# Fusion attention: the normalised input written by VectorE in one subtract-and-multiply, in place of ScalarE's scaled identity and GpSimd's product

## The chip, the core and the metric

The kernel runs on one core of a Trainium2 chip. The metric is the device time of one execution in microseconds. Engines are named as in the profile: PE (TensorE), with PEld for its weight loads, DVE (VectorE), ACT (ScalarE), POOL (GpSimd), SP (SyncE, which here only issues transfers).

## The reference

A batch of 64 samples. Each gives 128 image rows and 77 text rows of 64 numbers, `h` of shape 64 x 205 x 64. Then one attention layer and one layer of experts are added to it:

```python
h = jnp.concatenate([image_branch(x), text_branch(x_txt)], axis=1)        # (64, 205, 64)
h = h + attn(_layernorm(h), Wq, bq, Wk, bk, Wv, bv, Wo, bo)
h = h + ffn(_layernorm(h), W1, b1, Wg, bg, Wd, bd)

def _layernorm(x, axis=-1, eps=1e-05):
    m = jnp.mean(x, axis=axis, keepdims=True)
    v = jnp.var(x, axis=axis, keepdims=True)
    return (x - m) / jnp.sqrt(v + eps)

def attn(x, ...):            # 4 heads of 16
    q, k, v = heads(x @ Wq.T + bq), heads(x @ Wk.T + bk), heads(x @ Wv.T + bv)
    a = softmax(einsum('bhnd,bhmd->bhnm', q, k) * 16 ** -0.5)
    out = einsum('bhnm,bhmd->bhnd', a, v).transpose(0, 2, 1, 3).reshape(B, N, C)
    return out.astype(bfloat16).astype(float32) @ Wo.T + bo
```

The change is in `_layernorm(h)` ahead of the attention layer, and nowhere else.

## The kernel before

Four stages follow one another, each with its own block of instruction streams: image branch, text branch, fusion attention, experts. All of `h` stays in SBUF, as `h_img` (128 rows x 64 samples x 64) and `h_txt` (77 rows).

Fusion attention (`fusion_attention`) handles one sample a step, in a software pipeline over 64 samples: step `n` works on four samples at once. Every engine has a `step` function, and the order in which the code stands there is the order in which the engine runs it; engines are held together by semaphores alone. In step `n`:

- sample `n+3` is normalised. DVE takes means and variances of the two tiles (128 image rows, 77 text rows) with `set_stats`: `at_mean_var`, then `at_neg_mean` and `at_var_eps`. POOL makes `at_rstd` by a power of -0.5 and `at_neg_mean_rstd`, the product of the two (`set_scale`). ACT writes `at_z` = h * rstd + (-mean * rstd), one instruction a tile (`norm_rows`, line 1517). ACT then copies `at_z` rounded into `at_xs` (L1838), and POOL writes the rest, `at_z` minus that (L1780).
- sample `n+2` is projected. PE turns `at_xs` into the bank `at_work`, ACT copies it to `at_xT` (L1819), PE multiplies by `at_wk` and `at_wq` (L1891, four projections, two banks). For each projection ACT cuts a low part, `at_qk_lo` (`part_lo`, L1802), and DVE takes it off again with the bias, `at_KF` twice and then `at_QF` twice (`cut_qk`, L1701). POOL spreads each `at_KF` over the heads as `at_KB` (L1774). PE projects V behind the first `at_QF` (`project_v`, L1899).
- sample `n+1` has its scores and their row maxima (`at_mpad`, L1683), turned by PE into `at_maxT`, from which DVE makes `at_QP` (`join_max`, L1691).
- sample `n` has its transposed scores (L1865), the exponentials `at_PT` (L1792, two of them), the weighted sum `at_outT` (L1912), copied by ACT as `at_oU` (L1830); sample `n-1` is projected by `at_wo` and added to `h`.

The places that matter are the middle of the step on ACT (`part_lo` 0 and 1, `norm_rows`, `at_oU`, `part_lo` 2 and 3) and on DVE (`cut_qk` 0 and 1, `join_max`, `cut_qk` 2 and 3), and PE's `project_v`, which waits for `qk_cut` of `cut_qk` 2. The steps run in a loop of two steps per pass.

Of the kernel before, what the change touches and what calls it, by code (L numbers as in the profile page):

```python
# [1459 lines left out]
def set_stats(dve, rows_of, mean_var, stats, neg_mean, var_eps, aggregated, var_ready, m, between=None):  # L1460

    for t, (_, n) in enumerate(TILES):
        dve.bn_stats(stats[0:n, t], rows_of(m, t))
    if between:
        between()
    dve.drain()
    for t, (_, n) in enumerate(TILES):
        last = dve.bn_aggr(mean_var[0:n, t], stats[0:n, t])  # L1468
    last.then_inc(aggregated, 1)
    dve.wait_ge(aggregated, m + 1)  # L1470
    dve.tensor_scalar(neg_mean[:], mean_var[:, :, 0], -1.0, None, ALU.mult)
    dve.tensor_scalar(var_eps[:], mean_var[:, :, 1], EPS, None, ALU.add).then_inc(var_ready, 1)


# [47 lines left out]
def fusion_attention(p, inputs, ident, rows_of):  # L1522
# [8 lines left out]
    with ExitStack() as ctx:  # L1531
        def sb(name, shape, dtype=F32):
            return ctx.enter_context(nc.sbuf_tensor("at_" + name, shape, dtype))
# [9 lines left out]

        stats, mean_var = sb("stats", [P, 2, 6]), sb("mean_var", [P, 2, 2])
        var_eps, rstd = sb("var_eps", [P, 2]), sb("rstd", [P, 2])
        neg_mean, neg_mean_rstd = sb("neg_mean", [P, 2]), sb("neg_mean_rstd", [P, 2])
        z = sb("z", [P, 2, D])
        xs = sb("xs", [P, 2, 2 * D], F32R)
        xT = sb("xT", [P, SEQP], F32R)
# [23 lines left out]
        with ExitStack() as setup:  # L1573
# [76 lines left out]
                        dve.tensor_scalar(cols[:, at + 2:at + 4], cols[:, at:at + 2], lo_rows[:, who:who + 1],  # L1650
                                          None, ALU.mult)

        aggregated, var_ready, rstd_ready, scale_ready, z_ready, x_hi, x_cut, x_turned, xT_set = (
            sem("aggregated"), sem("var_ready"), sem("rstd_ready"), sem("scale_ready"), sem("z_ready"), sem("x_hi"),
            sem("x_cut"), sem("x_turned"), sem("xT_set"))
        projected, lo_part, qk_cut, k_split, v_made, v_set = (
            sem("projected"), sem("lo_part"), sem("qk_cut"), sem("k_split"), sem("v_made"), sem("v_set"))
# [16 lines left out]
        with nc.Block() as block:  # L1674
            @block.vector
            def _(dve):
                def find_max(m, tile):

                    n = TILES[tile][1]
                    dve.wait_ge(scored, m * 2 + (tile + 1))  # L1680
                    if tile == 0 and due(m):
                        dve.wait_ge(max_turned, m)
                    dve.tensor_reduce(mpad[0:n, tile].rearrange("p t (j r) -> p t j r", r=A_GROUP)[:, :, :, 3 * A_DH],  # L1683
                                      scores[0:n, :, 0:A_HPT * SEQP].rearrange("p t (j s) -> p t j s", j=A_HPT)[:, :, :, 0:SEQ],
                                      AX.X, ALU.max, negate=True).then_inc(max_set, 1)

                def join_max(m, par):
                    dve.wait_ge(max_turned, m + 1)
                    if due(m * 2 - 2):
                        dve.wait_ge(scored_t, m * 2 - 2)  # L1690
                    dve.tensor_tensor(QP[:, par, :, 0:SEQ], maxT[:, :, 0:SEQ], QF[:, par, :, 0:SEQ].bitcast(F32),  # L1691
                                      ALU.add).then_inc(q_set, 1)

                def cut_qk(m, i, par):

                    t, is_q = i % 2, i // 2
                    dst = QF[:, par, t] if is_q else KF[:, t]
                    dve.wait_ge(lo_part, m * 4 + (i + 1))
                    if i == 0 and due(m * 2):
                        dve.wait_ge(k_split, m * 2)  # L1700
                    dve.scalar_tensor_tensor(out=dst, in0=work[(i + 1) % 2][:, 0:SEQP],  # L1701
                                             scalar=cols[:, (0 if is_q else 4) + t:(1 if is_q else 5) + t],
                                             in1=qk_lo[:, i % 2].bitcast(F32), op0=ALU.add, op1=ALU.subtract)\
                        .then_inc(qk_cut, 1)

                def set_v(m, par):
                    dve.wait_ge(v_made, m + 1)
                    if due(m - 1):
                        dve.wait_ge(weighed, m - 1)
                    for tile, (_, n) in enumerate(TILES):  # L1710
                        last = dve.tensor_tensor(
                            V[0:n, par, tile, :, 0:A_DH],
                            work[1][0:n, tile * D:(tile + 1) * D].rearrange("p (h c) -> p h c", h=A_HEADS),
                            bv[0:n].rearrange("p (h c) -> p h c", h=A_HEADS), ALU.add)
                    last.then_inc(v_set, 1)

                def normalise_o(m, par):
                    dve.wait_ge(outs_turned, m + 1)
                    if due(m - 1):
                        dve.wait_ge(o_turned, m - 1)  # L1720
                    dve.reciprocal(rsum[:], outs[:, :, :, A_DH]).then_inc(sums_inv, 1)
                    dve.wait_ge(sums_inv, m + 1)
                    dve.tensor_tensor(o_rows[:, par, :, 0:D].rearrange("p a (h c) -> p a h c", h=A_HEADS), outs[:, :, :, 0:A_DH],
                                      rsum[:].unsqueeze(3).broadcast_to([P, 2, A_HEADS, A_DH]), ALU.mult)\
                        .then_inc(o_set, 1)

                def add_y(m):
                    dve.wait_ge(y_made, m + 1)
                    for tile, (_, n) in enumerate(TILES):
                        last = dve.tensor_tensor(rows_of(m, tile), rows_of(m, tile),  # L1730
                                                 work[1][0:n, tile * D:(tile + 1) * D], ALU.add)
                    last.then_inc(y_added, 1)

                def step(n, par):
                    if live(n + 3):
                        if due(n + 3):
                            dve.wait_ge(scale_ready, n + 3)
                        set_stats(dve, rows_of, mean_var, stats, neg_mean, var_eps, aggregated, var_ready, n + 3,
                                  between=(lambda: find_max(n + 1, 0)) if live(n + 1) else None)
                    elif live(n + 1):  # L1740
                        find_max(n + 1, 0)
                    if live(n - 1):
                        add_y(n - 1)
                    if live(n + 1):
                        find_max(n + 1, 1)
                    if live(n + 2):
                        cut_qk(n + 2, 0, par)
                        cut_qk(n + 2, 1, par)
                    if live(n + 1):
                        join_max(n + 1, 1 - par)  # L1750
                    if live(n + 2):
                        cut_qk(n + 2, 2, par)
                        cut_qk(n + 2, 3, par)
                    if live(n):
                        normalise_o(n, par)
                    if live(n + 2):
                        set_v(n + 2, par)

                each_step(dve, step)

            @block.gpsimd
            def _(pool):
                def step(n, par):
                    if live(n + 3):
                        set_scale(pool, neg_mean, var_eps, power, rstd, neg_mean_rstd, var_ready, rstd_ready,
                                  scale_ready, n + 3)
                    if live(n + 2):

                        m = n + 2
                        if due(m * 2 - 2):  # L1770
                            pool.wait_ge(scored_t, m * 2 - 2)
                        for t in range(A_TENSORS):
                            pool.wait_ge(qk_cut, m * 4 + (t + 1))
                            pool.tensor_tensor(KB[:, par, t],  # L1774
                                               KF[:, t].bitcast(F32).unsqueeze(1).broadcast_to([P, A_HPT, SEQP]),
                                               head_rows[:].unsqueeze(2).broadcast_to([P, A_HPT, SEQP]), ALU.mult)\
                                .then_inc(k_split, 1)
                    if live(n + 3):
                        pool.wait_ge(x_hi, n + 4)
                        pool.tensor_tensor(xs[:, :, D:], z[:], xs[:, :, 0:D].bitcast(F32), ALU.subtract)\  # L1780
                            .then_inc(x_cut, 1)

                each_step(pool, step)

            @block.scalar
            def _(act):
# [18 lines left out]
                def step(n, par):  # L1805
# [9 lines left out]
                    if live(n + 2):  # L1815
# [3 lines left out]
                        act.activation(xT[:, 0:SEQ], work[0][:, 0:SEQ], ACT.Copy).then_inc(xT_set, 1)  # L1819
                        part_lo(n + 2, 0)  # L1820
                        part_lo(n + 2, 1)
                    if live(n + 3):
                        if due(n + 3):
                            act.wait_ge(x_cut, n + 3)
                        norm_rows(act, rows_of, z, rstd, neg_mean_rstd, scale_ready, z_ready, n + 3)
                    if live(n):
                        act.wait_ge(weighed, n + 1)
                        if due(n):
# [577 lines left out]
```

## Time and profile before

| | us |
|---|---|
| median of 3 runs | 2744.31 |
| lowest, highest | 2728.9, 2755.52 |
| the profiled execution | 2730.05 |
| its span, first to last instruction | 2728.2 |
| attention stage, first to last exponential and what lies about it | 1832 to 2316 |
| busy over the whole span: PE, DVE, ACT, POOL | 2268.2, 1892.6, 1453.0, 1243.7 |
| mean granted clock of PE | 0.905 |

The profile is of one execution, near the lowest of the three runs. A stretch's granted clock is a mean between 0.5 (1.2 GHz) and 1 (2.4 GHz). Busy times don't add up to the span since engines work side by side; what sets a stage's time has to be read from its waits.

### The profile page before, as it was taken

What the parts mean: (1) busy time and instruction counts of PE and PEld (TensorE: products, weight loads), DVE (VectorE), ACT (ScalarE), POOL (GpSimd) and SP (SyncE); (2) the same over time, 40 slices, a digit from 0 to 9 for tenths busy, and PEclk for the clock granted to TensorE, in tenths of its full rate; (3) what the DMA queues carried; (4) which work ended last, traced back from release to release, by engine and by line L of the source; (5) the groups of instructions that cost most, each with busy time, mean ns of one, the idle gap of its engine ahead of it and who ended that gap; (6) DMA issues with size and microseconds to landing.
All of it is one profiled execution on the core that took longest, in us unless ns stands there. A gap on an engine that the chain in (4) does not pass through costs nothing. (4 is left out here: it accounts for less than half of the span.)

```text
span 2728.2 us, 63210 instructions
## 1 busy us (share of the span) xinstructions
PE 2268.2 (83%) x19769; PEld 1792.5 (66%) x19769; DVE 1892.6 (69%) x6491; ACT 1453.0 (53%) x3500; POOL 1243.7 (46%) x1650
## 2 busy tenths in 40 slices
PE   5699999778886998778877888628888898699998
PEld 5699999666665776656665666526666665466665
DVE  3455565467866777668856776668888766588888
ACT  2122222136656665756665665746666656566663
POOL 2233333226646555656555654664444433434442
PEclk8899999869978999989987998859999969699999
DMA  4100000000000000000000000000000000000000
GB/s 118 29 13 16 12 17 6 1 1 1 0 1 1 2 0 0 1 3 0 0 1 2 1 0 1 1 0 0 0 0 0 0 0 0 4 10 9 8 9 11
DMA packets 38122, 19.09 MB, mean 7 GB/s; under 512 B 28045, under 2 KB 37389, under 8 KB 37903
## 3 DMA queue, kind: packets, MB, share of 16 engines
q1 hardware_dynamic: 38003, 17.64, 2.6%
q8 instruction: 58, 0.95, 0.2%
q14 instruction: 61, 0.50, 0.1%
HBM read 14.27 MB, written 3.36 MB: 6 GB/s over the span
## 5 line engine op out<-in xcount | busy, mean ns | idle before, releaser
L444 PE MATMUL im_c<-im_a_hi,im_w 128*128 128x256 f32 (+2 forms) x1920 | 428.9, 318 | 47.0 <-POOL im_a_lo L341 47.0
L444 PEld LDWEIGHTS im_c<-im_a_hi,im_w 128*128 128x128 f32 x1920 | 321.2, 191 | 63.5 <-POOL im_a_lo L341 47.8
L1012 POOL TENSOR_TENSOR tx_KB<-tx_KF,tx_head_rows 128x1248 fp32r<-128x1248 f32 x128 | 288.1, 2271 | 52.1 <-DVE tx_KF L881 52.1
L444 PE MATMUL im_c<-im_a_lo,im_w 128*128 128x256 f32 (+2 forms) x960 | 304.1, 317 | 0.0
L830 POOL TENSOR_TENSOR tx_rstd<-tx_var_eps,tx_power 77x4 f32<-77x4 f32 x128 | 130.7, 1021 | 366.0 <-DVE tx_var_eps L826 366.0
L1080 ACT ACTIVATE tx_PT<-tx_scores_t 77x624 f32<-77x624 f32 x256 | 174.7, 682 | 219.1 <-PE tx_scores_t L1224 214.5
L1224 PE MATMUL tx_scores_t<-tx_QP,tx_KB 128*77 128x78 f32 x2048 | 206.5, 254 | 11.3 <-DVE tx_QP L901 6.3
L895 DVE TENSOR_REDUCE tx_mpad<-tx_scores 77x8 fp32r<-77x616 f32 x256 | 202.1, 790 | 11.2 <-PE tx_scores L1206 10.6
L1224 PEld LDWEIGHTS tx_scores_t<-tx_QP,tx_KB 128*77 128x77 f32 x2048 | 188.3, 161 | 30.8 <-DVE tx_QP L901 30.8
L334 POOL TENSOR_TENSOR im_rstd<-im_var_eps,im_power 128x4 f32<-128x4 f32 x64 | 68.7, 1074 | 304.7 <-DVE im_var_eps L262 304.7
L837 ACT ACTIVATE tx_yn<-tx_y,tx_neg_mean_rstd,tx_rstd 77x64 f32<-77x64 f32 x512 | 189.0, 433 | 6.7 <-POOL tx_neg_mean_rstd L832 6.7
L444 PEld LDWEIGHTS im_c<-im_a_lo,im_w 128*128 128x128 f32 x960 | 182.5, 190 | 8.3
L257 DVE BATCH_NORM_STATS2 im_stats<-im_h 128x6 f32<-128x128 f32 (+1 forms) x192 | 47.7, 304 | 185.0 <-ACT im_h L383 66.6
L2284 PE MATMUL ex_y<-ex_wd,ex_H_hi 128*128 128x512 f32 (+1 forms) x512 | 172.7, 419 | 0.0
L1073 ACT ACTIVATE tx_qk_lo<-tx_work,tx_cols,tx_lo_rows 128x312 fp32r<-128x312 f32 x258 | 143.1, 606 | 53.9 <-PE tx_work L1188 53.9
L1792 ACT ACTIVATE at_PT<-at_scores_t 128x824 f32<-128x824 f32 (+1 forms) x128 | 109.5, 856 | 106.3 <-PE at_scores_t L1865 106.3
L375 ACT ACTIVATE im_a_hi<-im_normed 128x192 fp32r<-128x192 f32 (+1 forms) x192 | 62.9, 348 | 192.9 <-DVE im_normed L280 190.9
L1774 POOL TENSOR_TENSOR at_KB<-at_KF,at_head_rows 128x412 fp32r<-128x412 f32 x128 | 109.3, 874 | 96.8 <-DVE at_KF L1701 96.8
L1683 DVE TENSOR_REDUCE at_mpad<-at_scores 128x4 fp32r<-128x820 f32 (+1 forms) x128 | 129.5, 1011 | 28.9 <-PE at_scores L1852 22.0
L1802 ACT ACTIVATE at_qk_lo<-at_work,at_cols,at_lo_rows 128x206 fp32r<-128x206 f32 x256 | 120.1, 519 | 54.6 <-PE at_work L1891 54.6
L1005 POOL TENSOR_TENSOR tx_xs<-h_txt,tx_xs 77x256 fp32r<-77x256 f32 x130 | 108.7, 836 | 70.6 <-ACT tx_xs L1061 68.9
L1179 PE MATMUL tx_work<-ident,tx_xs 128*128 128x128 f32 x516 | 92.9, 307 | 56.3 <-POOL tx_xs L1005 56.3
(286 smaller groups left out, 6027.1 us busy)
## 6 DMA issues: line engine op xcount, KB each, us to landing
im_x<-x SPq DMA_DIRECT2D x16, 384.0 KB, 3.4
out<-h_img SPq DMA_DIRECT2D x32, 64.0 KB
tx_toks<-x_txt SPq DMA_DIRECT2D x1, 1925.0 KB
im_raw<-L_tok_conv_w SPq DMA_DIRECT2D x1, 1280.0 KB, 8.7
out<-h_txt SPq DMA_DIRECT2D x32, 38.5 KB
im_raw<-L_tok_conv_w SPq DMA_DIRECT2D x1, 960.0 KB, 4.7
im_raw<-L_tok_conv_w SPq DMA_DIRECT2D x1, 640.0 KB, 5.9
tx_raw_W<-L_txt_W SPq DMA_DIRECT2D x2, 256.0 KB, 6.2
```

Source lines behind the costliest of these rows:

```text
L444: last = pe.matmul(acc[:, :, d0:d1], w[c][:, slot, part], img[:, b0_:b1_, d0 + shift:d1 + shift, kj:kj + J], start=opens, stop=closes)
L830: pool.tensor_tensor(rstd[:, par], var_eps[:, par], power[0:R], ALU.pow).then_inc(y_rstd, 1)
L837: last = act.activation(yn[:, par, b], y[:, par, b], ACT.Identity, bias=neg_mean_rstd[:, par, b:b + 1], scale=rstd[:, par, b:b + 1])
L895: dve.tensor_reduce(mpad[0:R].rearrange("p t (j r) -> p t j r", r=GROUP)[:, :, :, 3 * DH], scores[0:R, :, 0:HPT * SP_TXT].rearrange("p t ( ...
L1012: pool.tensor_tensor(KB[:, par, t], KF[:, t].bitcast(F32).unsqueeze(1).broadcast_to([P, HPT, QW]), head_rows[:].unsqueeze(2).broadcast_to( ...
L1073: act.activation(qk_lo[:, i % 2], work[(i + 1) % 2][:, 0:QW], ACT.Identity, bias=cols[:, at:at + 1], scale=lo_rows[:, 1 - is_q:2 - is_q]). ...
L1080: act.activation(PT[0:R, b % 2], scores_t[0:R, :, 0:HPT * SP_TXT], ACT.Exp, scale=SCALE)\
L1224: last = pe.matmul(scores_t[0:R, t, j * SP_TXT:(j + 1) * SP_TXT], k, QP[:, b % 2, t], start=True, stop=True)
L1683: dve.tensor_reduce(mpad[0:n, tile].rearrange("p t (j r) -> p t j r", r=A_GROUP)[:, :, :, 3 * A_DH], scores[0:n, :, 0:A_HPT * SEQP].rearra ...
L1792: act.activation(PT[0:n, tile], scores_t[0:n, :, 0:A_HPT * SEQP], ACT.Exp, scale=SCALE)\
L1802: act.activation(qk_lo[:, i % 2], work[(i + 1) % 2][:, 0:SEQP], ACT.Identity, bias=cols[:, at:at + 1], scale=lo_rows[:, 1 - is_q:2 - is_q] ...
L2284: last = pe.matmul(acc, h[:, slot, half, at:at + n], wd[:, part, half, 0:WIDE], start=False, stop=half == HALVES - 1 and h is H_lo)
```

## The change

DVE writes `at_z` with one TENSOR_SCALAR a tile: subtract the mean, multiply by `at_rstd`, both operands columns with one value a row. It stands in a new function `norm_z`, called behind `cut_qk(n + 2, 1, par)` and ahead of `join_max(n + 1, 1 - par)`. ACT's two instructions for `at_z` go, and so do POOL's `at_neg_mean_rstd`, DVE's `at_neg_mean` and the semaphore `scale_ready` in this stage. The experts stage still uses the old functions.

```diff
@@ set_stats
     dve.wait_ge(aggregated, m + 1)
-    dve.tensor_scalar(neg_mean[:], mean_var[:, :, 0], -1.0, None, ALU.mult)
+    if neg_mean is not None:
+        dve.tensor_scalar(neg_mean[:], mean_var[:, :, 0], -1.0, None, ALU.mult)
     dve.tensor_scalar(var_eps[:], mean_var[:, :, 1], EPS, None, ALU.add).then_inc(var_ready, 1)
@@ fusion_attention, DVE
+                def norm_z(m):
+                    dve.wait_ge(rstd_ready, m + 1)
+                    if due(m):
+                        dve.wait_ge(x_cut, m)
+                    for t, (_, n) in enumerate(TILES):
+                        last = dve.tensor_scalar(z[0:n, t], rows_of(m, t), mean_var[0:n, t, 0:1], rstd[0:n, t:t + 1],
+                                                 ALU.subtract, ALU.mult)
+                    last.then_inc(z_ready, 1)
@@ DVE, step
                     if live(n + 3):
-                        if due(n + 3):
-                            dve.wait_ge(scale_ready, n + 3)
-                        set_stats(dve, rows_of, mean_var, stats, neg_mean, var_eps, aggregated, var_ready, n + 3,
+                        set_stats(dve, rows_of, mean_var, stats, None, var_eps, aggregated, var_ready, n + 3,
                                   between=(lambda: find_max(n + 1, 0)) if live(n + 1) else None)
...
                         cut_qk(n + 2, 0, par)
                         cut_qk(n + 2, 1, par)
+                    if live(n + 3):
+                        norm_z(n + 3)
                     if live(n + 1):
                         join_max(n + 1, 1 - par)
@@ POOL, step
                     if live(n + 3):
-                        set_scale(pool, neg_mean, var_eps, power, rstd, neg_mean_rstd, var_ready, rstd_ready,
-                                  scale_ready, n + 3)
+                        pool.wait_ge(var_ready, n + 4)
+                        pool.tensor_tensor(rstd[:], var_eps[:], power[:], ALU.pow).then_inc(rstd_ready, 1)
@@ ACT, step
                         part_lo(n + 2, 0)
                         part_lo(n + 2, 1)
-                    if live(n + 3):
-                        if due(n + 3):
-                            act.wait_ge(x_cut, n + 3)
-                        norm_rows(act, rows_of, z, rstd, neg_mean_rstd, scale_ready, z_ready, n + 3)
                     if live(n):
                         act.wait_ge(weighed, n + 1)
```

DVE's order in the middle of a step of the loop, before. `at_KF` comes from `cut_qk` 0 and 1, `at_QP` from `join_max`, `at_QF` from `cut_qk` 2 and 3:

```order
L1468 BN_AGGR at_mean_var<-at_stats 77x2
L1471 TENSOR_SCALAR at_neg_mean<-at_mean_var 128x2
L1472 TENSOR_SCALAR at_var_eps<-at_mean_var 128x2
L1730 TENSOR_TENSOR h_img<-h_img,at_work 128x64
L1730 TENSOR_TENSOR h_txt<-h_txt,at_work 77x64
L1683 TENSOR_REDUCE at_mpad<-at_scores 77x4
L1701 SCALAR_TENSOR_TENSOR at_KF<-at_work,at_cols,at_qk_lo 128x206 x2
L1691 TENSOR_TENSOR at_QP<-at_maxT,at_QF 128x2x205
L1701 SCALAR_TENSOR_TENSOR at_QF<-at_work,at_cols,at_qk_lo 128x206 x2
```

And the same place of DVE in the changed kernel:

```order
L1701 SCALAR_TENSOR_TENSOR at_KF<-at_work,at_cols,at_qk_lo 128x206
L1722 TENSOR_SCALAR at_z<-h_img,at_mean_var,at_rstd 128x64
L1722 TENSOR_SCALAR at_z<-h_txt,at_mean_var,at_rstd 77x64
L1690 REGISTER_ALU
L1691 TENSOR_TENSOR at_QP<-at_maxT,at_QF 128x2x205
```

The two `at_z` now stand on DVE between the second `at_KF` and `at_QP`, and `at_neg_mean` is gone ahead of `at_var_eps`.

ACT's order at the same place of a step, before; `at_qk_lo` is `part_lo`:

```order
L1802 ACTIVATE at_qk_lo<-at_work,at_cols,at_lo_rows 128x206
L1515 REGISTER_ALU
L1517 ISA
L1517 ACTIVATE at_z<-h_img,at_neg_mean_rstd,at_rstd 128x64
L1517 REGISTER_ALU
L1517 ACTIVATE at_z<-h_txt,at_neg_mean_rstd,at_rstd 77x64
L1827 REGISTER_ALU
L1830 ACTIVATE at_oU<-at_outT 128x206
```

And in the changed kernel:

```order
L1811 ACTIVATE at_qk_lo<-at_work,at_cols,at_lo_rows 128x206
L1832 REGISTER_ALU
L1835 ACTIVATE at_oU<-at_outT 128x206
L1808 REGISTER_ALU
L1811 ACTIVATE at_qk_lo<-at_work,at_cols,at_lo_rows 128x206
```

On ACT `at_oU` follows the second `at_qk_lo` directly.

## Rows read from the trace of the kernel before

**Rows 1.** Windows of the attention stage: stretch, length, busy time, granted clock, DMA.

```profile
1832.00:2180.00 348.00, 292.64 (x2550) 212.50 (x2550) 282.41 (x898) 238.74 (x567) 143.99 (x236) 0.98 0.00 0
2180.00:2316.00 136.00, 120.71 (x867) 88.00 (x866) 91.92 (x284) 81.20 (x183) 44.52 (x72) 0.76 0.00 0
```

**Rows 2.** Waits, 1832 to 2316: total us, times, longest.

```profile
POOL at_KB L1774 <- DVE at_KF L1701: 94.3, 62, 4.8
...
PE at_work L1899 <- DVE at_QF L1701: 27.4, 62, 0.6
```

**Rows 3.** Timeline: start us, us, engine, line, instructions; one step.

```profile
2071.36 0.58 DVE L1691 TENSOR_TENSOR at_QP<-at_maxT,at_QF 128x410 fp32r<-128x410 f32 x1
...
2076.35 0.70 PE L1891 MATMUL at_work<-at_xT,at_wk 128*128 128x206 f32 x4 [0.27 <-ACT at_xT L1819]
...
2076.94 0.94 ACT L1802 ACTIVATE at_qk_lo<-at_work,at_cols,at_lo_rows 128x206 fp32r<-128x206 f32 x2 [0.64 <-PE at_work L1891]
...
2077.59 0.77 DVE L1701 SCALAR_TENSOR_TENSOR at_KF<-at_work,at_cols,at_qk_lo 128x206 fp32r<-128x206 f32 x2 [0.46 <-ACT at_qk_lo L1802]
2077.77 0.43 ACT L1517 ACTIVATE at_z<-h_img,at_neg_mean_rstd,at_rstd 128x64 f32 x1
...
2078.10 1.71 POOL L1774 TENSOR_TENSOR at_KB<-at_KF,at_head_rows 128x412 fp32r<-128x412 f32 x2 [1.38 <-DVE at_KF L1701]
2078.10 0.43 ACT L1517 ACTIVATE at_z<-h_txt,at_neg_mean_rstd,at_rstd 77x64 f32 x1
...
2078.17 0.71 PE L1891 MATMUL at_work<-at_xT,at_wq 128*128 128x206 f32 x4
2078.43 0.32 ACT L1830 ACTIVATE at_oU<-at_outT 128x206 f32<-128x206 f32 x1
2078.50 0.58 DVE L1691 TENSOR_TENSOR at_QP<-at_maxT,at_QF 128x410 fp32r<-128x410 f32 x1
2078.66 0.94 ACT L1802 ACTIVATE at_qk_lo<-at_work,at_cols,at_lo_rows 128x206 fp32r<-128x206 f32 x2
...
2079.22 0.84 DVE L1701 SCALAR_TENSOR_TENSOR at_QF<-at_work,at_cols,at_qk_lo 128x206 fp32r<-128x206 f32 x2
...
2079.71 0.55 PE L1899 MATMUL at_work<-at_wv,at_xT 128*128 128x64 f32 x4 [0.46 <-DVE at_QF L1701]
```

**Rows 4.** Like operations on DVE: a source view of L288, L699; timeline of L288.

```profile
L288 DVE TENSOR_SCALAR im_res<-im_h,im_mean_var,im_rstd x64: 339/342/347, 104.9 to 531.1; 128x128 f32<-128x128 f32 x64
...
L699 DVE TENSOR_SCALAR tx_hot<-tx_toks,tx_word_f x16: 367/367/372, 549.6 to 566.2; 100x308 f32 x14, 100x308 f32<-100x308 int32 x2
...
104.94 1.11 DVE L288 TENSOR_SCALAR im_res<-im_h,im_mean_var,im_rstd 128x128 f32<-128x128 f32 x4 [1.12 <-POOL im_rstd L334]
```

**Rows 5.** Source view of L1774: ns min/median/max.

```profile
L1774 POOL TENSOR_TENSOR at_KB<-at_KF,at_head_rows x128: 869/874/877, 1822.3 to 2305.0; 128x412 fp32r<-128x412 f32 x128
```

**Rows 6.** Source view of L825; timeline at 1117 us, DVE and POOL.

```profile
L825 DVE TENSOR_SCALAR tx_neg_mean<-tx_mean_var x128: 166/166/447, 611.8 to 1762.2; 77x4 f32<-77x4 f32 x128
...
1117.53 0.45 DVE L825 TENSOR_SCALAR tx_neg_mean<-tx_mean_var 77x4 f32<-77x4 f32 x1
...
1117.21 0.73 POOL L843 TENSOR_TENSOR tx_x_shift<-h_txt,tx_rows 77x256 f32<-77x256 f32 x1
```

**Rows 7.** Timeline at 32 us, DVE and POOL.

```profile
32.07 1.01 DVE L280 SCALAR_TENSOR_TENSOR im_normed<-im_scaled,im_rstd,im_b 128x192 f32<-128x192 f32 x2
...
32.30 2.15 POOL L341 TENSOR_TENSOR im_a_lo<-im_normed,im_a_hi 128x192 fp32r<-128x192 f32 x4 [1.24 <-ACT im_a_hi L375]
```

**Rows 8.** Timeline at 862 us, DVE and POOL.

```profile
862.13 0.16 DVE L826 TENSOR_SCALAR tx_var_eps<-tx_mean_var 77x4 f32<-77x4 f32 x1
...
862.12 0.75 POOL L1005 TENSOR_TENSOR tx_xs<-h_txt,tx_xs 77x256 fp32r<-77x256 f32 x1 [1.93 <-ACT tx_xs L1061]
```

**Rows 9.** Timeline of DVE in a stretch at half clock.

```profile
2241.09 0.59 DVE L1691 TENSOR_TENSOR at_QP<-at_maxT,at_QF 128x410 fp32r<-128x410 f32 x1
...
2248.44 0.77 DVE L1701 SCALAR_TENSOR_TENSOR at_KF<-at_work,at_cols,at_qk_lo 128x206 fp32r<-128x206 f32 x2 [0.30 <-ACT at_qk_lo L1802]
2250.61 0.58 DVE L1691 TENSOR_TENSOR at_QP<-at_maxT,at_QF 128x410 fp32r<-128x410 f32 x1 [1.40 <-PE at_maxT L1927]
2251.55 0.86 DVE L1701 SCALAR_TENSOR_TENSOR at_QF<-at_work,at_cols,at_qk_lo 128x206 fp32r<-128x206 f32 x2 [0.36 <-ACT at_qk_lo L1802]
```

More of the change, by code:

```diff
@@ L1545, in fusion_attention @@
         var_eps, rstd = sb("var_eps", [P, 2]), sb("rstd", [P, 2])
-        neg_mean, neg_mean_rstd = sb("neg_mean", [P, 2]), sb("neg_mean_rstd", [P, 2])
         z = sb("z", [P, 2, D])
@@ L1651, in _ @@
                                           None, ALU.mult)
-        aggregated, var_ready, rstd_ready, scale_ready, z_ready, x_hi, x_cut, x_turned, xT_set = (
-            sem("aggregated"), sem("var_ready"), sem("rstd_ready"), sem("scale_ready"), sem("z_ready"), sem("x_hi"),
+        aggregated, var_ready, rstd_ready, z_ready, x_hi, x_cut, x_turned, xT_set = (
+            sem("aggregated"), sem("var_ready"), sem("rstd_ready"), sem("z_ready"), sem("x_hi"),
             sem("x_cut"), sem("x_turned"), sem("xT_set"))
```

## The prediction

> **What bounds the kernel now.** Only the attention stage changes, so I read that stretch first, by the view of windows: from 1832 to 2316 us, 484 of the 2728.2, PE is busy 84% in the part at full clock and 89% in the part where the clock was partly granted at half, DVE 81% and 68%, ACT 69% and 60%, POOL 41% and 33% [rows 1]. No engine is full, so busy shares decide nothing: the stage is a cycle of waits. The view of waits shows two of its links, PE waiting for `at_QF` before the V projection 62 times, once a step, 27.4 us in all, and POOL idle 94.3 us before `at_KB` [rows 2].
>
> The timeline of one step gives the cycle [rows 3]. Two `at_QP` starts, 2071.36 and 2078.50, give its period, 7.14 us; the step that also closes the loop takes 7.36, by the same reading. Inside it PE's K projection starts at 2076.35, ACT's first `at_qk_lo` at 2076.94, DVE's `at_KF` pair at 2077.59, the `at_QF` pair at 2079.22, and PE's V projection at 2079.71, half a microsecond after `at_QF` began, with PE idle before it. Behind it PE issues in order the transposed scores, on which ACT's exponentials and the next `at_xT` wait. So whatever moves the start of `at_QF` moves the whole step.
>
> What holds `at_QF` now is ACT: `at_qk_lo` starts at 2078.66 and lasts 0.52 (two in 0.94), and `at_QF` starts 0.04 after its end. Just before it ACT runs without a gap: `at_qk_lo` pair, `at_z`, `at_z`, `at_oU`, `at_qk_lo` [rows 3]. Both rows of `at_z` are thus on the path as the row stands, which makes the change look like a gain. DVE's `at_QP` ends at 2079.08, 0.14 us before `at_QF`.
>
> **The change part by part.** ACT loses two `at_z` of 0.43 us, which start 0.33 apart: 0.66 us less in front of `at_qk_lo` [rows 3]. That buys nothing, because PE stands right behind. The third `at_qk_lo` needs the Wq projection, which starts at 2078.17, 0.49 us before it. For the first `at_qk_lo` the same distance is 0.59 us (2076.35 to 2076.94). PE itself issued Wq behind its own transposes. The bound from above is therefore 0 us, and from below a few hundredths; I take 0. POOL loses `at_neg_mean_rstd`, 0.20 us, at a time when it waits anyway: 0. DVE loses `at_neg_mean`, 0.17 us, in front of a `at_mpad` that waits for PE's scores: 0. The wait for `scale_ready` at the head of DVE's step had always been met: 0.
>
> DVE gains two TENSOR_SCALAR of 64 columns with two column operands, between the `at_KF` pair and `at_QP`. The nearest row is `im_res`, the same operation with 128 columns: 342 ns, four in 1.11 us, so (1.11 - 0.34) / 3 = 0.257 us apart [rows 4]. This class of operation takes in about two columns a cycle: `tx_hot` writes 308 columns in 367 ns, where `at_KF` needs 430 for 206 [rows 3, 4]. 64 columns fewer are 0.033 us less: an estimate of 0.31 us each, 0.22 apart. If nothing else held them, the first would start at 2078.27 (two `at_KF` of 0.43 in 0.77 us start 0.34 apart, so the second did at 2077.93, and the next can 0.34 later), the second at 2078.49, `at_QP` at 2078.71 in place of 2078.50, ending at 2079.29; back-to-back operations overlap by 0.08 to 0.09, so `at_QF` could start at 2079.21. Against 2079.22 that is nothing. This is the lower end.
>
> But they would not be alone. POOL begins the first `at_KB` at 2078.10, at the end of the first `at_KF`, and the two run to 2079.81 [rows 3]; one lasts 874 ns [rows 5], so the first ends at 2078.97. The trace shows what a TENSOR_SCALAR from SBUF to SBUF does while POOL works: `tx_neg_mean`, 166 ns at the median of 128, took 447 when it started 0.32 us into a 0.73 us product on POOL, and ended 0.04 us after that product, at 1117.98 against 1117.94 [rows 6]. So DVE stands still until POOL's instruction is over. The `at_z` pair comes inside `at_KB` in every step, because `at_KB` is released by the first `at_KF` and `at_z` by the second.
>
> How many of the two `at_KB` does it wait for? In the image part DVE's `im_normed` ran into four `im_a_lo` that POOL issues without a gap (32.30 to 34.45, 0.54 each) and had ended by 33.08, while the second was under way [rows 7]: a waiting DVE instruction slips in between two of POOL's. So the first `at_z` runs at 2078.97, ending at about 2079.03 (0.04 as there, and some 0.03 for the columns). The second has to be ready before POOL takes hold again. `tx_var_eps`, which started 0.01 us behind a POOL product, was not held (0.16 us) [rows 8]; so POOL takes hold about 0.15 us after its start, which here is 2078.93 + 0.15 = 2079.08. The second `at_z` is ready 0.22 after the first, at 2079.2: too late by 0.1 us. I take it to wait for the second `at_KB`, to 2079.81, and to end at 2079.87. `at_QP` follows at 2079.79 (overlap 0.08), ends at 2080.37, and `at_QF` starts at 2080.29 in place of 2079.22: **1.07 us a step**, all of it on the cycle.
>
> Beside these rows: the Trainium skill, SBUF — State Buffer, section Who interferes with whom, says that a `tensor_scalar` in a two-port mode and a GpSimd operation exclude one another, that whichever issued first keeps the pair of ports for its whole instruction, and that the other is fully blocked. No row here shows it for column operands. By the page's order of issue (first `at_z`, second `at_KB`, second `at_z`) the sum is 1.07 us as well; by busy times alone it would be 0.
>
> How many steps pay? Both sides of the wait are there in 62 steps [rows 2]. In the part at half clock PE is so late that the wait is covered: there `at_KF` starts at 2248.44, so `at_KB` would end 2.2 us later (as in rows 3) at 2250.66, while `at_QP` started only at 2250.61 behind PE's transposes, and `at_QF` at 2251.55 behind ACT [rows 9]. A step there costs 0 more. From 2180 to 2316 the mean clock was 0.76, which is 48% of 136 us, 65 us, at 1.2 GHz, and 0.98 over 348 us adds 14 [rows 1]; at about 10 us a step (2241.09 to 2250.61 is 9.5) that is 8 steps. 62 - 8 = 54 steps, by 1.07: **58 us**. Against the profiled execution's own 2730.05 us (span 2728.2 and 1.9 around it) that gives 2788. The three runs have their median 14 us higher, at 2744.31; put on that, 2802. I forecast 2800.
>
> **Rivals.**
> - *Not slower: DVE isn't held.* Column operands, or the strided `h_img` rows, might keep `at_z` on one port. Then `at_QF` starts at 2079.21 and nothing moves: 2744. For it: no row shows `im_res` under a POOL instruction. Against it: its 342 ns fit two columns a cycle, the class that was held. It decides below 0.2 us of waiting per step, the slack found above.
> - *Both slip in.* If POOL takes hold 0.1 us later than I read, both `at_z` end by 2079.25; `at_QP` starts at 2079.17, `at_QF` at 2079.67: 0.45 us by 54, 24 us, 2768.
> - *Both wait for the second `at_KB`.* 1.07 + 0.22 = 1.29 us by 54, 70 us: 2814.
> - *The clock gives back.* The mean granted clock was 0.98 up to 2180, with PE busy 84%, and stretches at 1.2 GHz came after that [rows 1]. With PE at 73% (84 by 7.25 / 8.32) these may not come: 62 steps pay 66 us, and 8 steps of 10 us fall back to 7.25, minus 22 to 24: +42, 2786.
> - *A gain.* It needs ACT's relief to reach `at_QF` and DVE to be free: at most 0.14 us by 62, 9 us, under the 1% (27 us) that a measurement of this kernel can tell.
>
> **How the numbers follow.** Main case 0.58, with the clock giving back 0.10, both waiting 0.07, both slipping in 0.10, not held 0.13, a gain 0.02. The range goes from 2755 (both slipping in, less half of the 27 us that the runs spread) to 2822 (both waiting, plus 8) and leaves out 0.15. Over 1% slower is above 2772: the first three cases and a little of the fourth, 0.77. Within 1%: 0.21. Faster by over 1%: 0.02.
>
> **What the changed profile would show.** DVE `at_z` with a median far above 0.31 us, the first ending 0.06 after the first `at_KB`, the second 0.06 after the second; `at_QP` to `at_QP` 8.2 and 8.4 us; ACT idle before its third `at_qk_lo` or right after it; PE idle over 1.5 us before the V projection in place of 0.46; POOL's `at_KB` still 874 ns. If both `at_z` last about 0.31 and steps stay at 7.14, the hold was misread. If one is short and one long the order in the gap is right. A different share of the half-speed clock would move the total by tens of microseconds without touching these.

## The result, and the profile after

The changed kernel takes 2857.65 us (median of 4 runs, 2853.64 to 2868.36), against 2736.61 for the kernel before (4 runs, 2724.39 to 2755.52): a ratio of 1.044, 95% interval 1.037 to 1.052. Every ratio here compares only the executions of each kernel that lie within 1.5% of its fastest, since the granted clock differs from one execution to the next. The kernel is slower, as forecast, but by 121 us where 56 were forecast, and above the range. The profiled execution, the slowest of the four, took 2868.36 us with a span of 2866.6, 138 us more than the span of before; the sums below are of the two profiled executions, and so add up to 138 and not to 121.

Where the time lies is read from windows. The view of one source line gives the stage's ends: the first and the last instruction of PE's output projection, which comes once a sample, start at 1845.8 and 2459.0 us, 613 us apart, where they started 475 apart before (1843.2 and 2318.6). The difference is 138 us, so all of it is in the attention stage. In the windows below (stretch, length, busy time of PE, PEld, DVE, ACT and POOL, granted clock) the stage's row answers to [rows 1]:

```profile
2097.40:2107.30 9.90, 6.82 (x64) 5.08 (x62) 8.86 (x25) 6.01 (x14) 4.11 (x7) 1.00 0.00 0
2107.50:2118.00 10.50, 10.25 (x56) 7.64 (x56) 7.56 (x22) 4.81 (x10) 2.51 (x4) 0.50 0.00 0
1832.00:2459.00 627.00, 576.64 (x3424) 426.47 (x3424) 459.86 (x1246) 301.83 (x628) 176.08 (x247) 0.60 0.00 0
```

The granted clock of the stage is 0.60, where [rows 1] had 0.98 and 0.76 for its two parts. At 0.60, 80% of 627 us, some 500 us, ran at 1.2 GHz. The first two rows are a little over one step at each level. The fall at the end of the first of them came just after PE had stood still for 1.6 us.

That step, at 2.4 GHz, answers to [rows 3]. DVE's rows first, then POOL's, ACT's and PE's of the same stretch:

```profile
2098.21 0.57 DVE L1691 TENSOR_TENSOR at_QP<-at_maxT,at_QF 128x410 fp32r<-128x410 f32 x1
...
2104.20 0.77 DVE L1701 SCALAR_TENSOR_TENSOR at_KF<-at_work,at_cols,at_qk_lo 128x206 fp32r<-128x206 f32 x2 [0.47 <-ACT at_qk_lo L1811]
2104.89 0.75 DVE L1722 TENSOR_SCALAR at_z<-h_img,at_mean_var,at_rstd 128x64 f32 x1
2105.55 0.91 DVE L1722 TENSOR_SCALAR at_z<-h_txt,at_mean_var,at_rstd 77x64 f32 x1
2106.38 0.57 DVE L1691 TENSOR_TENSOR at_QP<-at_maxT,at_QF 128x410 fp32r<-128x410 f32 x1
2106.88 0.76 DVE L1701 SCALAR_TENSOR_TENSOR at_QF<-at_work,at_cols,at_qk_lo 128x206 fp32r<-128x206 f32 x2
...
2104.71 1.70 POOL L1783 TENSOR_TENSOR at_KB<-at_KF,at_head_rows 128x412 fp32r<-128x412 f32 x2 [1.73 <-DVE at_KF L1701]
...
2105.27 0.94 ACT L1811 ACTIVATE at_qk_lo<-at_work,at_cols,at_lo_rows 128x206 fp32r<-128x206 f32 x2 [0.38 <-PE at_work L1896]
...
2107.35 0.86 PE L1904 MATMUL at_work<-at_wv,at_xT 128*128 128x64 f32 x4 [1.63 <-DVE at_QF L1701]
```

The first `at_z` lasts 0.75 us and ends at 2105.64; the second lasts 0.91 and ends at 2106.46, 0.05 us after the pair of `at_KB`, which ends at 2106.41. `at_QF` starts 2.68 us after the first `at_KF`; in [rows 3] it was 1.63. That is 1.05 us, and the step from `at_QP` to `at_QP` is 8.17 us in place of 7.14. PE's idle time ahead of the V projection is 1.63 us in place of 0.46. From one V projection to the next (2099.17 to 2107.35) PE is busy 5.83 of 8.18 us, 71%. ACT waits 0.38 us for PE ahead of its third `at_qk_lo`, with both of its `at_z` gone.

The next step ran at 1.2 GHz and answers to [rows 9]:

```profile
2114.11 0.77 DVE L1701 SCALAR_TENSOR_TENSOR at_KF<-at_work,at_cols,at_qk_lo 128x206 fp32r<-128x206 f32 x2 [0.30 <-ACT at_qk_lo L1811]
2114.80 0.75 DVE L1722 TENSOR_SCALAR at_z<-h_img,at_mean_var,at_rstd 128x64 f32 x1
2115.47 0.91 DVE L1722 TENSOR_SCALAR at_z<-h_txt,at_mean_var,at_rstd 77x64 f32 x1
2116.30 0.57 DVE L1691 TENSOR_TENSOR at_QP<-at_maxT,at_QF 128x410 fp32r<-128x410 f32 x1
2117.22 0.86 DVE L1701 SCALAR_TENSOR_TENSOR at_QF<-at_work,at_cols,at_qk_lo 128x206 fp32r<-128x206 f32 x2 [0.35 <-ACT at_qk_lo L1811]
```

Both `at_z` are held as long, and it costs nothing: `at_QF` starts 3.11 us after `at_KF`, as in [rows 9] (2248.44 to 2251.55), and waits for ACT. A step from `at_QP` to `at_QP` that is wholly at 1.2 GHz lasts about 10.3 us (2155.01 to 2165.32). Some 500 us of these are about 48 steps, where the kernel before had 8 or so.

### The profile page after: what moved, and what is told of

Read it like the earlier page. It is cut to its first block and busy times, and to the rows that moved or that the text cites. A ratio compares the mean times of both kernels' runs of the same rounds, so it can differ in the third digit from the quotient of the medians.

```text
span 2866.6 us, 62995 instructions
## 1 busy us (share of the span) xinstructions
PE 2427.9 (85%) x19769; PEld 1915.5 (67%) x19769; DVE 1983.1 (69%) x6555; ACT 1431.0 (50%) x3372; POOL 1228.4 (43%) x1586
## 5 line engine op out<-in xcount | busy, mean ns | idle before, releaser
L906 DVE RECIPROCAL tx_rsum<-tx_out_bank 77x8 f32<-77x8 f32 x256 | 51.6, 201 | 132.1 <-PE tx_out_bank L1244 125.1
```

## The experiments

The time of the stage below is always from the first to the last start of the output projection: 475 us before, 613 us changed.

**1. `at_z` on DVE ahead of `at_KF`.** At that place POOL has nothing to do and DVE waits for ACT anyway.

```diff
                     if live(n + 1):
                         find_max(n + 1, 1)
+                    if live(n + 3):
+                        norm_z(n + 3)
                     if live(n + 2):
                         cut_qk(n + 2, 0, par)
                         cut_qk(n + 2, 1, par)
-                    if live(n + 3):
-                        norm_z(n + 3)
```

> The changed kernel with the two at_z moved on DVE from behind the second at_KF to ahead of the first, where POOL does nothing. Theory (DVE is held by POOL's at_KB, and the pause this opens in PE's work takes the full clock away): both at_z last 0.31 us, steps at full clock last 7.1 to 7.4 us, the mean granted clock of the attention stage is 0.9 or more, and the time is 2720 to 2750 us. Rival one (the two more instructions on DVE cost, held or not): at_z short, but a time over 2770. Rival two (the clock falls because ACT or POOL work was taken off or because the kernel's rhythm changed, not by the pause): at_z short, but a granted clock near 0.6 in the stage and a time over 2800.

Measured: 2821.21 us (2808.01 to 2845.61), ratio 1.039 (1.031 to 1.046). The first rows are of one tile, `at_z` (ns minimum, median, maximum); then one step of the timeline at 2.4 GHz; then windows:

```profile
L1722 DVE TENSOR_SCALAR at_z<-h_img,at_mean_var,at_rstd x64: 301/301/314, 1813.8 to 2370.6; 128x64 f32 x58, 128x64 f32<-128x64 f32 x6
L1722 DVE TENSOR_SCALAR at_z<-h_txt,at_mean_var,at_rstd x64: 302/305/307, 1814.0 to 2370.9; 77x64 f32 x58, 77x64 f32<-77x64 f32 x6
...
1897.46 0.72 PE L1896 MATMUL at_work<-at_xT,at_wq 128*128 128x206 f32 x4
1897.79 0.58 DVE L1691 TENSOR_TENSOR at_QP<-at_maxT,at_QF 128x410 fp32r<-128x410 f32 x1
1897.95 0.94 ACT L1811 ACTIVATE at_qk_lo<-at_work,at_cols,at_lo_rows 128x206 fp32r<-128x206 f32 x2 [0.38 <-PE at_work L1896]
1898.02 0.38 PE L1925 MATMUL at_outT<-ident,at_oU 128*128 128x128 f32 x2
1898.51 0.84 DVE L1701 SCALAR_TENSOR_TENSOR at_QF<-at_work,at_cols,at_qk_lo 128x206 fp32r<-128x206 f32 x2
...
1899.00 0.30 PE L1904 MATMUL at_work<-at_wv,at_xT 128*128 128x64 f32 x1 [0.60 <-DVE at_QF L1701]
...
1826.00:2401.00 575.00, 518.48 (x3428) 381.97 (x3427) 404.68 (x1255) 298.09 (x631) 180.13 (x263) 0.69 0.00 0
```

No `at_z` is held any more. ACT's third `at_qk_lo` starts 0.49 us after the Wq projection, the very distance of [rows 3], though ACT had stood idle: ACT's relief buys nothing on the path, PE stands right behind it. The steps at 2.4 GHz last 7.36 and 7.14 us, as before. And yet the stage takes 555 us (1841.2 to 2396.4), 80 more than before, with the clock at 0.69. So the hold alone doesn't explain the loss, and my theory that only the pause opened by the hold takes the clock away fell here: the second rival came nearer. What differs from the kernel before at 2.4 GHz is small. `at_oU` and with it PE's transposes (L1925) start 0.56 us after Wq, where they started 0.64 after it before (2078.17 to 2078.81 in the trace of before), PE's idle time ahead of the V projection is 0.60 us in place of 0.46 [rows 3], and PE is busy 81% of a stretch at 2.4 GHz (26.55 of 33 us, 1890 to 1923), where it was 83% before (33.32 of 40 us, 1900 to 1940).

**2. The same DVE order as the changed kernel, but POOL waits.** The first `at_KB` comes only after `at_z`.

```diff
                         for t in range(A_TENSORS):
+                            if t == 0 and live(n + 3):
+                                pool.wait_ge(z_ready, n + 4)
                             pool.wait_ge(qk_cut, m * 4 + (t + 1))
```

> The changed kernel, in which POOL's first at_KB also waits for z_ready, so that at_z on DVE comes before both at_KB and never beside one. DVE's order is that of the changed kernel. Theory of the hold: both at_z last 0.31 us, at_QF starts about 1.6 us after the first at_KF, at_KB ends some 0.75 us later than before, which its reader in the next step (the scores) can just stand: 2725 to 2765 us. Rival (the place in DVE's order costs, not the hold): a step over 8 us and a time over 2800.

Measured: a median of 2738.68 us over ten runs that lie from 2721.05 to 2840.05, against 2728.61 for the kernel before on the same chip (13 runs, 2709.09 to 2767.69). The ratio is 1.000 (0.996 to 1.004), but it rests on six of the ten runs; over all runs the mean is 2760 us, against 2731 for the kernel before. The two `at_z` last 306 and 304 ns at the median. The spread goes with the clock: 0.909 at 2721.05 us, 0.904 at 2730.24, 0.872 at 2790.90 and 0.843 at 2840.05. The hold is gone at DVE's place of the changed kernel too, and how much of the time runs at 1.2 GHz varies from run to run.

The profiled execution (2744.46 us) also bears on experiment 1. Its stage takes 489 us (1846.4 to 2335.1), 13 more than before. PE's row first, then a stretch at 2.4 GHz and the stage:

```profile
1897.25 0.55 PE L1906 MATMUL at_work<-at_wv,at_xT 128*128 128x64 f32 x4 [0.59 <-DVE at_QF L1701]
...
1888.50:1921.50 33.00, 27.41 (x241) 20.03 (x239) 27.39 (x90) 20.93 (x46) 13.37 (x19) 1.00 0.00 0
1832.00:2330.00 498.00, 432.36 (x3401) 313.07 (x3400) 389.40 (x1242) 295.41 (x629) 175.23 (x249) 0.88 0.00 0
```

ACT is relieved as in experiment 1, the transposes come as early (0.56 us after Wq, 1895.71 to 1896.27), and PE's pause is as long, 0.59 us at the median of the steps at 2.4 GHz. Yet the stage kept a clock of 0.88 where experiment 1 had 0.69. So neither the relief nor the length of this pause decides alone. PE's busy share in such a stretch is 83% here against 81% there.

**3. Only the second `at_KB` waits** (the same lines with `t == 1`).

> The changed kernel, in which only POOL's second at_KB waits for z_ready. The first at_z is still held by the first at_KB (0.75 us), the second follows at once (0.31 us). at_QF starts about 2.1 us after the first at_KF, 0.45 later than before. Steps at full clock 7.6 and 7.8 us. If the clock stayed as in the kernel before: 2755 to 2770 us. Theory that the pause in PE's work takes the clock: part of the stage falls to half clock, 2770 to 2840 us. It tells how long the pause has to be.

Measured: 2825.67 us (2818.29 to 2837.25), ratio 1.038 (1.032 to 1.045). The medians of `at_z` are 748 and 302 ns: the first is held by the first `at_KB`, and with the second `at_KB` kept back the second is free. This is what both slipping in would have looked like. Up to 2400 us its clock was 0.70. `at_QF` starts 2.07 us after the first `at_KF` (2010.41 to 2012.48) in place of 1.63. That delay, under half of the changed kernel's, costs 97 us, where experiment 4, which has the whole delay on the same chip, lost 137. So the clock isn't lost in proportion to the pause.

**4. The kernel before, with the two instructions on DVE beside ACT's own `at_z`.** They write to a scratch tile that nothing reads.

```diff
+                    if live(n + 3):
+                        dve.wait_ge(rstd_ready, n + 4)
+                        for t, (_, rows) in enumerate(TILES):
+                            dve.tensor_scalar(z2[0:rows, t], rows_of(n + 3, t), mean_var[0:rows, t, 0:1],
+                                              rstd[0:rows, t:t + 1], ALU.subtract, ALU.mult)
                     if live(n + 1):
                         join_max(n + 1, 1 - par)
```

> The kernel before, with at_z still made by ACT, plus the two instructions of the change on DVE at the same place, writing to a scratch tile that nothing reads. ACT, POOL and every wait between engines are as before. Theory (hold by at_KB, then clock): as the changed kernel, the two last 0.75 and 0.91 us, full-clock steps 8.2 us, clock of the stage near 0.6, time 2840 to 2870 us. Rival (the loss comes from what ACT or POOL no longer do, or from ACT's at_xs that waits for DVE): a time within 1% of before.

Measured: 2865.51 us (2856.13 to 2869.65), ratio 1.051 (1.045 to 1.057).

```profile
L1753 DVE TENSOR_SCALAR at_z<-h_img,at_mean_var,at_rstd x64: 314/746/748, 1819.1 to 2428.6; 128x64 f32 x58, 128x64 f32<-128x64 f32 x6
L1753 DVE TENSOR_SCALAR at_z<-h_txt,at_mean_var,at_rstd x64: 305/908/911, 1819.4 to 2429.2; 77x64 f32 x58, 77x64 f32<-77x64 f32 x6
...
1832.00:2459.00 627.00, 567.78 (x3429) 418.79 (x3428) 470.54 (x1320) 338.99 (x754) 191.56 (x324) 0.62 0.00 0
```

The whole loss is there with ACT and POOL as before. (The program gives the scratch tile the name of `at_z`; ACT's own rows stand at L1517.)

**5. The kernel before, with a pause on DVE of another kind.** A reduction over 1380 columns of a constant tile stands between `at_KF` and `at_QP`; its result is not read.

```diff
+                    if live(n + 3):
+                        dve.tensor_reduce(pause_out[:], pause[:], AX.X, ALU.max)
                     if live(n + 1):
                         join_max(n + 1, 1 - par)
```

> The kernel before, plus one reduction on DVE between at_KF and at_QP over 1380 columns of a constant SBUF tile (about 1.5 us, its result is not read). No at_z on DVE, nothing new from SBUF to SBUF in the form that POOL held, ACT and POOL unchanged. at_QF starts about 1.05 us later in a step at full clock, as in the changed kernel. If the delay of DVE is all that matters, whatever makes it: steps of 8.2 us at full clock, a granted clock near 0.6 in the attention stage, 2840 to 2870 us. Rival (the waiting on POOL's port does something beyond the delay): clearly less, near 2790 us with the clock at 0.9.

Measured: 2858.54 us (2856.65 to 2864.06), ratio 1.051 (1.041 to 1.062). The reduction lasts 1.58 us beside `at_KB` and never more than 1.582.

```profile
1832.00:2454.00 622.00, 566.39 (x3408) 417.69 (x3406) 467.83 (x1245) 335.94 (x748) 190.15 (x321) 0.61 0.00 0
```

A delay of the same length (the two `at_z` together take 1.57 us) without any hold gives the same time and the same clock as experiment 4. The hold acts by its delay alone, as far as these two runs can tell.

**6. The changed kernel, with PE kept busy.** The two transposes of `at_oU`, which come right ahead of the V projection, are done six times over.

```diff
                 def turn_outs(m):
                     pe.wait_ge(out_copied, m + 1)
-                    for tile, (at, n) in enumerate(TILES):
+                    for tile, (at, n) in list(enumerate(TILES)) * 6:
```

> The changed kernel, in which PE does its two transposes of at_oU six times over in place of once (the same values to the same place, five pairs more, about 1.3 us at full clock), which fills its idle time ahead of the V projection. Theory (the hold costs 1.07 us a step at full clock, 60 to 66 us in all, and the rest of the loss is the clock that falls after PE's idle time): the clock of the stage goes back to 0.9 or more, steps 8.2 and 8.4 us, time 2780 to 2800 us, faster than the changed kernel although it does more. Rival (the clock falls for another reason, PE's load in all): no higher clock, and steps at half clock of over 12 us: 2900 us or more.

Measured: 2779.35 us (2774.26 to 2786.62), a little under the 2780 to 2800 expected, and 78 us less than the changed kernel with 640 more matmuls. Against the kernel before, a ratio of 1.023 (1.012 to 1.033), where the changed kernel had 1.044; the kernel before was 21 us faster beside this experiment (2716.01) than beside the changed kernel, so not all of the 78 need be the transposes. The stages of the two profiled executions differ by 90 us (613 to 523). DVE's timeline, then PE's of the same steps, then the stage's window:

```profile
1879.51 0.57 DVE L1691 TENSOR_TENSOR at_QP<-at_maxT,at_QF 128x410 fp32r<-128x410 f32 x1
1887.93 0.57 DVE L1691 TENSOR_TENSOR at_QP<-at_maxT,at_QF 128x410 fp32r<-128x410 f32 x1
1896.11 0.57 DVE L1691 TENSOR_TENSOR at_QP<-at_maxT,at_QF 128x410 fp32r<-128x410 f32 x1
...
1886.88 1.48 PE L1925 MATMUL at_outT<-ident,at_oU 128*128 128x128 f32 x12
1888.89 0.55 PE L1904 MATMUL at_work<-at_wv,at_xT 128*128 128x64 f32 x4 [0.54 <-DVE at_QF L1701]
...
1832.00:2371.00 539.00, 458.29 (x4047) 355.54 (x4046) 452.13 (x1246) 292.88 (x626) 177.93 (x260) 0.95 0.00 0
```

PE's idle time of 1.63 us is 0.54, the clock is 0.95, and the steps are 8.42 and 8.18 us, the predicted ones. This is nearly the hold by itself.

**7. Experiment 1, with the transposes done twice.**

> The kernel with at_z on DVE ahead of at_KF, in which PE does its two transposes of at_oU twice over, one pair more (about 0.27 us at full clock, within 0.60 us of idle time). Theory (taking at_z off ACT lets at_oU and PE's transposes go earlier, which joins PE's idle time ahead of the V projection from 0.46 into one pause of 0.60 us, and the clock falls after it): clock of the stage 0.9 or more, steps 7.1 and 7.4 us, 2700 to 2740 us. Rival (the clock falls for another reason): 2820 us or more.

Measured: 2706.14 us (ten runs, 2700.46 to 2715.61), ratio to the kernel before 0.997 (0.9935 to 1.0004). Against experiment 1 that is 115 us less for one more pair of transposes a step (the kernel before differed by 13 between the two).

```profile
2002.22 0.60 PE L1925 MATMUL at_outT<-ident,at_oU 128*128 128x128 f32 x4
2003.20 0.55 PE L1904 MATMUL at_work<-at_wv,at_xT 128*128 128x64 f32 x4 [0.38 <-DVE at_QF L1701]
...
1832.00:2286.00 454.00, 384.17 (x3492) 285.74 (x3491) 394.72 (x1229) 283.62 (x619) 175.26 (x245) 0.99 0.00 0
```

**8. The kernel before, with the transposes done twice.**

> The kernel before, in which PE does its two transposes of at_oU twice over (about 0.27 us at full clock, within 0.46 us of idle time ahead of the V projection). If PE's idle time there is what lets the clock fall, the 65 us at half clock that the attention stage has in the kernel before go as well: about 20 us less, 2700 to 2715 us. Rival: no change of the clock and a step 0 to 0.1 us longer, 2728 to 2740 us.

Measured: 2706.10 us (ten runs, 2698.35 to 2710.47), ratio 0.997 (0.993 to 1.001); the kernel before beside it had a median of 2716.01 in 19 runs from 2702.45 to 2822.59. PE idles 0.24 us ahead of the V projection (2063.51 us) in place of 0.46.

```profile
1832.00:2293.00 461.00, 391.35 (x3499) 287.25 (x3498) 374.19 (x1179) 310.92 (x738) 187.30 (x317) 0.99 0.00 0
```

The stage takes 453 us (1833.9 to 2286.6). The kernel before is itself near the edge; what the added pair gives is above all the narrow spread, 12 us in place of 120.

**9. Experiment 8, with two reductions on DVE at the place of the changed kernel's `at_z`,** over the 64 columns of the same rows of `h`.

> The kernel before with PE's transposes of at_oU done twice (as in the run that keeps the clock up), plus two reductions on DVE over the 64 columns of the same two tiles of h, at the place of at_z in the changed kernel; their results are not read. They read SBUF beside at_KB like at_z, but are of a kind (TENSOR_REDUCE) that no row shows held by POOL. Theory (only what POOL holds costs): both about 0.2 us, not longer beside at_KB, steps 7.15 and 7.36 us, 2700 to 2712 us. Rival (any two more instructions of DVE at this place cost 0.2 us a step or more): 2718 us or more.

Measured: 2709.70 us (2705.45 to 2712.33), ratio 0.9965 (0.993 to 1.000). The source view gives the two reductions:

```profile
L1752 DVE TENSOR_REDUCE at_row_max<-h_img x64: 208/210/214, 1816.9 to 2278.6; 128x1 f32 x58, 128x1 f32<-128x64 f32 x6
L1752 DVE TENSOR_REDUCE at_row_max<-h_txt x64: 201/205/208, 1817.1 to 2278.7; 77x1 f32 x58, 77x1 f32<-77x64 f32 x6
```

In a step of the timeline they start at 2003.38 and 2003.50, beside an `at_KB` that runs from 2003.20. Two more instructions that read SBUF there are not held, and the stage takes 455 us (1845.6 to 2301.0), 3 more than in experiment 8. So it isn't every read of SBUF that POOL holds up: a TENSOR_SCALAR is held and a TENSOR_REDUCE isn't.

**10. Experiment 2, with the transposes done twice.**

> The changed kernel in which POOL's first at_KB waits for z_ready, now with PE's transposes of at_oU done twice to keep the clock up. at_z stands in DVE's order where the change puts it. Without hold and with the clock the place itself should cost what the steps of the first run of this kind at full clock showed over those of before, about 0.1 us a step: 2705 to 2725 us, in a narrower spread than that run's 2721 to 2840. If it is over 2750 the place in DVE's order has a price of its own beside the hold.

Measured: 2710.14 us (2707.02 to 2712.13), ratio 0.995 (0.991 to 0.999), the ten runs 5 us apart where experiment 2's were 119. `at_z` lasts 307 and 304 ns. The stage takes 458 us (1841.0 to 2298.6). With the clock held, the change at its own place in DVE's order, but never beside `at_KB`, costs 5 us of the stage against experiment 8; by their ratios, 0.995 and 0.997, the two can't be told apart.

## Why the prediction was right and wrong, point by point

- **DVE is held by POOL, the first `at_z` slips in between the two `at_KB`, the second waits for the second.** Right. 0.75 and 0.91 us, ends 0.06 and 0.05 us after the first and second `at_KB`; `at_QF` 1.05 us later by the trace, 1.07 forecast. Experiments 2 and 3 take the hold away from both and from one; 5 shows that it acts by its delay, and 9 that a reduction at the same place is not held. The Trainium skill, SBUF — State Buffer, section Who interferes with whom, states this exclusion and its order of issue; the trace agrees, now for column operands too.
- **ACT's relief buys nothing.** Right for the path (0.49 us behind Wq in experiment 1 too). The whole is open: with the relief and no hold, experiment 1 lost 80 us of its stage to the clock, and experiment 2, relieved as much, lost 13. In experiment 4 ACT is not relieved, and the whole loss is there.
- **62 steps, 8 of them covered.** This is the step that failed: "62 - 8 = 54 steps, by 1.07". The count of steps at half clock was taken over from the kernel before. It was about 48 after. They pay nothing for the hold but 3.1 us each for the clock (10.3 against about 7.25), so the term was of the wrong kind rather than a little off. As an estimate, 14 steps by 1.07 are 15 us, and 40 more steps at 1.2 GHz by 3.1 are 124: 139, where the stage measured 138. The 10 us of a step at half clock were read too low as well: the step of [rows 9] began at 2.4 GHz (2241.09 to 2244.50 has a granted clock of 1.00).
- **"The clock gives back."** This rival had the wrong sign. I argued that a PE which is less busy would be less throttled. With PE at 71% in a full-clock step (5.83 of 8.18 us), near the 73% forecast, the clock fell; and in experiments 6, 7, 8 and 10, in which PE does more, it stayed at 0.95 to 0.99.
- **The sum in another way.** By the stage's times: hold 523.0 (experiment 6) - 452.7 (experiment 8) = 70 us, forecast 58, or 66 for all 62 steps, so right; the 70 include what the clock of 0.95 in experiment 6 still costs. Clock 613.2 - 523.0 = 90 us, less the 475.4 - 452.7 = 23 that the kernel before lost already. Together, before rounding, 70 + 90 - 23 = 138 us, the measured difference; forecast for the clock was 0. The 23 us of before were in view, at 22 to 24 in the working of that rival; the 90 were not. That the direction came out right is due to the hold, which was forecast.

What of this is shown and what is argued: that more work of PE at this place keeps the clock, and that a delay of DVE at this place loses it, is shown (5, 6, 7, 8). Why experiment 1 loses the clock is not. Its pause of PE grew by 0.14 us over the kernel before, but experiment 2 has the same pause and mostly kept the clock. PE's busy share over the whole step fell too, and the added pairs of transposes raise that share as they shorten the pause, so these runs don't separate the two. A run that moves `at_oU` back without adding work was not made.

## What to carry to other kernels

Before moving a copy-like operation to DVE, look at what POOL does at that moment: on this chip a TENSOR_SCALAR from SBUF to SBUF waits until POOL's instruction is over, so two operations of 0.3 us, which had room in the step, cost 1.05; put it where POOL idles, or use a form that isn't held. A cycle of waits in which PE idles for some tenths of a microsecond in every step can lose TensorE's full clock by a delay that looks harmless, here more than the delay itself; so a delay on such a path has two prices, and the second is to be asked for with its own row, the granted clock of the stage. If a kernel's runs spread by several per cent on one core, try a few redundant matmuls in PE's idle time: here they took 10 us off the median of the kernel before (though its ratio, 0.997, is within the noise), 78 off the changed one and 115 off experiment 1.

## What the hardware showed that was not expected

- TensorE stays at 1.2 GHz for several steps though PE is busy almost without a gap: 10.25 of 10.50 us in the step shown, with 0.23 us of idle time ahead of the V projection, and 75.25 of 77 us from 2149 to 2226 us of the changed kernel, at a granted clock of 0.50 throughout. Why it stays there is not shown.
- The edge between the two levels is narrow. The same code (experiment 2) ran in 2721 us once and in 2840 another time, with granted clocks of 0.909 and 0.843 over the whole kernel; one pair of transposes a step (experiment 10) put all ten runs within 5 us.
- Times of ACT, POOL and DVE don't move with it: the first pair of `at_qk_lo` takes 0.94 us, the pair of `at_KB` 1.70, the two `at_z` 0.75 and 0.91, at both levels.
